# Interleaving key and value matmuls over two accumulation banks in a cross-attention projection

## What is computed

```python
qh = (q @ Wq.T).reshape(B, Lq, H, D).transpose(0, 2, 1, 3)
kh = (k @ Wk.T).reshape(B, Lk, H, D).transpose(0, 2, 1, 3)
vh = (v @ Wv.T).reshape(B, Lk, H, D).transpose(0, 2, 1, 3)
qh = _layernorm(qh, gq, bq) * scale
kh = _layernorm(kh, gk, bk)
attn = jax.nn.sigmoid(jnp.einsum('bhqd,bhkd->bhqk', qh, kh))
x = jnp.einsum('bhqk,bhkd->bhqd', attn, vh)
```

## Time and profile before

| | |
|---|---|
| median of 3 runs | 2914.47 us (2910.73 to 2915.18) |
| span of the profiled execution | 2914.7 us |
| PE busy | 2831.7 us, 97% of the span |
| DVE busy | 1466.7 us, 50% |
| ACT busy | 1464.8 us, 50% |
| POOL busy | 891.6 us, 31% |

### The profile page before, as it was taken

How to read it: one execution, slowest core, us unless ns; L and a number is a source line. 1 busy time by engine, 2 the same in 40 slices (tenths; PEclk the granted TensorE clock), 3 DMA queues, 4 the chain that set the end, 5 groups by cost and what they waited for, 6 DMA issues and landing times.

```text
span 2914.7 us, 68560 instructions
## 1 busy us (share of the span) xinstructions
PE 2831.7 (97%) x27730; PEld 2271.9 (78%) x27730; DVE 1466.7 (50%) x2158; ACT 1464.8 (50%) x1450; POOL 891.6 (31%) x615
## 2 busy tenths in 40 slices
PE   4999999999999999999999999977999999999999
PEld 3777777777777777777777777736999998999998
DVE  5444444444444444444444444447577765667754
ACT  0555555555545555555555555523546565646554
POOL 2444444444444444444444444410000000000000
PEclk8999999999999999999999999988999999999999
DMA  5333233333333332233333333212545555545453
GB/s 209 84 86 86 80 83 86 82 81 85 86 82 81 85 86 80 83 86 86 80 82 86 83 81 84 76 37 87 180 169 193 181 188 192 199 174 202 179 189 131
DMA packets 194480, 334.46 MB, mean 115 GB/s; under 512 B 21736, under 2 KB 122344, under 8 KB 173040
## 3 DMA queue, kind: packets, MB, share of 16 engines
q1 hardware_dynamic: 194416, 333.56, 36.7%
HBM read 281.57 MB, written 51.90 MB: 114 GB/s over the span
## 4 chain that ended last, share of the span: by engine, by line
PE 80%; DVE 6%; issue 4%; DMA 4%; POOL 4%; SPq 1%; ACT 1%; DVEq 0%; POOLq 0%; ACTq 0%
PE kv_ps L1091 30%; PE f_ps L1330 23%; PE s_ps L1116 10%; PE o_ps L1128 9%; PE y_ps L1314 5%; POOL k_var L462 2%; DMA k_rows<-k_dram 2%; DMA k_dram<-k_blocks 2%; DVE k_n L737 1%; POOL ctx_lo L452 1%; SPq L383 1%; PE pm L1197 1%; DVE w_lo L668 1%; DVE k_blocks L741 1%; DVE v_sb L726 1%
## 5 line engine op out<-in xcount | busy, mean ns | idle before, releaser
L518 ACT ACTIVATE even_probs<-s_ps 128x2048 f32<-128x2048 f32 x196 | 369.0, 1883 | 506.6 <-PE o_ps L1128 344.4
L462 POOL TENSOR_TENSOR k_var<-k_var,neg_half 128x16 f32<-128x16 f32 x196 | 579.7, 2958 | 15.4 <-POOL k_var L458 0.2
L518 ACT ACTIVATE odd_probs<-s_ps 128x2048 f32<-128x2048 f32 x196 | 369.8, 1887 | 193.8 <-PE s_ps L1116 193.8
L668 DVE TENSOR_TENSOR w_lo<-w_raw,w_hi 128x2048 fp32r<-128x2048 f32 x160 | 366.5, 2292 | 173.4 <-ACT w_hi L558 173.3
L452 POOL TENSOR_TENSOR ctx_lo<-ctx_raw,ctx_hi 128x512 fp32r<-128x512 f32 x196 | 252.9, 1290 | 599.3 <-DVE ctx_hi L711 599.3
L1330 PE MATMUL f_ps<-h_hi,w_hi 128*128 128x256 f32 x1536 | 429.1, 279 | 0.0
L1330 PE MATMUL f_ps<-h_lo,w_hi 128*128 128x256 f32 x1536 | 428.1, 279 | 0.0
L1330 PE MATMUL f_ps<-h_hi,w_lo 128*128 128x256 f32 x1536 | 428.1, 279 | 0.0
L730 DVE TENSOR_REDUCE k_var<-k_sq 128x16 f32<-128x512 f32 x196 | 134.5, 686 | 508.3 <-ACT k_sq L524 508.3
L558 ACT ACTIVATE w_hi<-w_raw 128x2048 fp32r<-128x2048 f32 x160 | 305.8, 1913 | 73.3 <-PE y_ps L1314 62.4
L1091 PE MATMUL kv_ps<-wk_hi,ctx_hi 128*128 128x512 f32 x784 | 329.2, 420 | 4.3 <-DVE q_lo L797 2.8
(11 more groups left out here) (196 smaller groups left out, 5031.3 us busy)
## 6 DMA issues: line engine op xcount, KB each, us to landing
w_raw<-w_dram SPq DMA_DIRECT2D x160, 1024.0 KB, 4.8
ctx_raw<-ctx_dram SPq DMA_DIRECT2D x196, 256.0 KB, 2.7
k_dram<-k_blocks SPq DMA_DIRECT2D x784, 64.0 KB, 1.7
k_rows<-k_dram SPq DMA_DIRECT2D x196, 256.0 KB, 2.9
qkv_w<-qkv_w_dram SPq DMA_DIRECT2D x1, 3072.0 KB, 13.8
bias_rows<-bias_rows_dram SPq DMA_DIRECT2D x1, 1280.0 KB, 16.5
wq<-wq_dram SPq DMA_DIRECT2D x1, 1024.0 KB, 5.5
wk_rows<-wk_dram SPq DMA_DIRECT2D x1, 1024.0 KB, 7.6
```

The lines of the kernel that those rows point to most:

```text
L462: g.tensor_tensor(k_var[:, 2], k_var[:, 1], neg_half[:].to_broadcast([P, H]), ALU.pow)\
L518: s.activation(probs[r % 2][half][:], s_ps[:], ACT.Sigmoid).then_inc(probs_made, 1)
L668: v.tensor_tensor(w_lo[i][:], w_raw[i % RAW][:], w_hi[i][:].bitcast(f32), ALU.subtract)\
```

## The change

In a full stretch the key and value matmuls now alternate, chunk by chunk and product by product, and so the two banks alternate. Both waits that used to stand ahead of the first key and the first value matmul stand ahead of the whole stretch. The two half stretches of tile r+1 (12 keys, 12 values) keep their order and their waits. No instruction is added or removed, on any engine.

```diff
             def projection(it, r, first, last):
 
+                if first == 0:
+                    pe.wait_ge(ctx_lo_made, n_of(it, r, 1, 1))
+                    wait(pe, k_kept, n_of(it, r))
+                if last == 24:
+                    wait(pe, v_copied, n_of(it, r))
+                if (first, last) == (0, 24):
+                    for c in range(CT):
+                        for n in range(3):
+                            for which in range(2):
+                                project(it, r, which, c, n)
+                    return
                 for m in range(first, last):
-                    if m == 0:
-                        pe.wait_ge(ctx_lo_made, n_of(it, r, 1, 1))
-                        wait(pe, k_kept, n_of(it, r))
-                    if m == 12:
-                        wait(pe, v_copied, n_of(it, r))
                     project(it, r, m // 12, m % 12 // 3, m % 3)
```

## The result

| | median, us | lowest to highest | runs |
|---|---|---|---|
| before | 2912.6 | 2909.1 to 2915.18 | 4 |
| changed | 3295.31 | 3294.36 to 3298.74 | 4 |

The ratio is 1.1312, with a 95% interval of 1.1293 to 1.1331: 13% slower. The forecast was 3130 us, range 3088 to 3148. The direction was right, the time outside the range by nearly 150 us.

What follows compares the result with a forecast made beforehand. The prediction took the loop as bound by PE's own instructions; 6.4 us at the head, 95 x 2.20 in the loop and 0.14 for the last keys made 215.5 us more, so 3130 us, range 3088 to 3148.

Steps and rivals of the forecast that it cites:

- The wait in front: Before each full stretch, PE waits for the values' copy: next stretch at T + 20.90, not T + 18.84, 2.06 us idle.
- The matmuls themselves: In the full stretch, alternating banks brings no gain and no loss; steps stay at 0.229 us.
- The late keys: Keys finish 2.49 us later in a full stretch; through POOL, DVE and the round trip, normalisation comes 0.14 us later.
- 21.04: The loop's forecast period in us, 18.98 + 2.06, which is 2.20 more than 18.84.
- The clock: Rival: PE's clock falls to 1.2 GHz after each wait, 1.87 us more per full stretch, 3308 us; chance 4%.
- The sum: Whole kernel: 6.4 + 95 x 2.20 + 0.14 = 215.5 us added, giving 3130 us.
- the head: Ahead of the loop: its first full stretch starts at 93.88 in place of 87.49, 6.4 us later.

Runs made afterwards that it cites:

- this edit alone: The kernel before with the wait for v_copied ahead of the full stretch, and 8 filler matmuls ahead of that wait: 3160.8 us, ratio 1.0837.
- the twelve fillers: The changed kernel with 12 extra key matmuls, their sums overwritten, ahead of each full stretch before the wait for v_copied: 3189.1 us, ratio 1.0953.
- the wait in front only: The kernel before with the wait for v_copied moved ahead of a full stretch's first matmul, all keys still before all values: 3215.9 us, ratio 1.1043.
- the split first: The changed kernel with split_keys of tile r-1 ahead of sum_squares of tile r on DVE: 3214.5 us, ratio 1.1045.

## Why the prediction was wrong

*The wait in front* was right in place and mechanism: the copy that stands behind the second tile's normalisation holds all 24 matmuls. At full clock, in the periods where POOL's power isn't held up, it makes 20.93 us, forecast 20.90; but with this edit alone only 24 of 95 periods are like that, and the mean is 21.34. That moving the copy takes away nearly all of the loss shows that it is the cause.

*The matmuls themselves* were right: alternating costs and gives nothing (18.84 us with it and without a wait).

*The late keys* were right in that they cost nothing alone (2914.5 us); whether their 0.14 us beyond the wait in front is there can't be told from the rest. The step that failed within it was "POOL's power ended at 1015.41 + 2.90 = 1018.31; 2.49 later it is T + 10.15", the duration of an instruction carried to a place where another engine works over its start. With the keys late, DVE does `split_keys` as the power starts, which then takes 3.34 us, and the addition 0.33 and not 0.21. From the square to the normalisation it is 5.23 us (1014.02 to 1019.25) where the forecast carried 4.68. The page "SBUF — State Buffer" of the Trainium skill, section "Who interferes with whom", says that a DVE instruction with two SBUF inputs contends with a GpSimd instruction that reads SBUF. `kt_lo` is such an instruction. The traces agree where it runs over the start of the power, 3.34 against 2.91 us, and not where it falls in the middle of it, 2.90 us. Those 0.55 us are nearly all of the step from 21.04 to the 21.65 of the twelve fillers; the rest is small (PE starts 0.18 us after the copy in the mean, not 0.06, and 0.06 us come off elsewhere). Together it is 0.61 us, 58 us over the loop.

*The clock* was the step that failed outright. The forecast dismissed the rival with "after the wait of 2.07 us that ended at 78.82 the granted clock was 1.00". One wait was taken for a rule. The kernels here show a share and not a bound: 65 of 96 stretches at half clock behind waits of 2.2 to 3.3 us, 42 behind 2.1 to 2.8, eight behind about 1.5 to 1.9, none behind less than 1.5. With the wait in front only, half-clock stretches stand behind waits from 2.13 us on, and 9 of 57 waits of 2.0 to 2.2 us were followed by one, so the forecast's 2.1 to 2.2 us were not safe even had the rest been right; the 2.85 us of the changed kernel, which POOL's longer power helped to make (2.38 in the mean with the split first), were worse. The price was sized well, 1.87 us in the forecast, 1.61 measured (6.93 against 5.32); how many stretches pay was not. It is 22.79 - 21.65 = 1.14 us in the mean period, 108 us over the loop. The rival's own 3308 us is close to the result by two errors that cancel: it let every stretch pay, and it too lacked POOL's part.

*The sum* then reads, on the spans: ahead of the loop 96.76 - 87.49 = 9.3 us (forecast 6.4; there too the power takes 3.34 us, so that tile 2's square to its normalisation is 5.64 and not 4.68, and its rows are back 7.74 us after the transpose and not 6.24), in the loop 95 x (22.79 - 18.84) = 375, and 7 us less after the last full stretch than before, which stays open: 378 in all, where the forecast had 215.5. Of the 162 us between them the clock makes 108, POOL's power and the small latencies 58, and the head 3, less the 7.

## What to carry to other kernels

When a wait moves ahead of a block of work, find what produces the thing waited for and what that instruction stands behind on its own engine: here a copy with its data ready stood behind a long chain, and moving two lines on DVE was worth more than any order on PE. Price new idle time on TensorE twice, once as idle and once as the slower matmuls that may follow, by the share of waits that are followed by a drop, and don't take one wait that wasn't as proof. A chain that moves in time meets other neighbours; a duration read in one place holds only while the engines beside it do the same at the same moment of it.

## What was not expected of the hardware

Idle times of 1.5 to 1.9 us on TensorE, after some 20 us of dense work, were now and then followed by six to eight steps of 0.43 us at the 1.2 GHz level; the slow steps do not always begin with the first matmul (at 1006.80 they begin with the third, in other stretches anywhere up to the seventh). Which stretches are hit goes by a beat, mostly two of three in the changed kernel, and not by the length of the wait alone: waits of 3.09 us went free and one of 1.54 us did not. What sets the beat stays open here. And useless matmuls, enough to fill a wait, took 106 us off a kernel. A two-input subtraction on DVE makes a small power on POOL 0.44 us longer when it runs over the power's start, and not at all when it falls in the middle: 3.34 against 2.90 us.
